# Graph attention on one core: scores laid out by unit, head and node, and gathers released unit by unit

## What is computed

```python
h = layer_norm(x, ln1_g, ln1_b)
xl = (h @ Wl + bl).reshape(n, HEADS, DIM)
xr = (h @ Wr + br).reshape(n, HEADS, DIM)
e = jax.nn.leaky_relu(xl[src] + xr[dst], NEG_SLOPE)
score = jnp.einsum('ehd,hd->eh', e, att)
smax = jax.ops.segment_max(score, dst, num_segments=n)
ex = jnp.exp(score - smax[dst])
alpha = ex / (segment_sum(ex, dst)[dst] + 1e-16)
g = segment_sum(xl[src] * alpha[..., None], dst)
x = x + (g.reshape(n, HEADS * DIM) + gat_b) @ proj_W + proj_b
x = x + gelu(layer_norm(x, ln2_g, ln2_b) @ W1 + b1) @ W2 + b2
```

## Time and profile before

| | |
|---|---|
| median of 3 runs | 3252.38 us (3250.22 to 3263.53) |
| span of the profiled execution, first to last instruction | 3186.6 us |
| median less span (what lies around the span) | 65.8 us |
| TensorE clock granted, mean | 0.897 |
| PE, weight loads, DVE, ACT, POOL busy | 77%, 50%, 45%, 43%, 48% |
| DMA | 334.02 MB, mean 105 GB/s |

### The profile page before, as it was taken

One profiled execution on the slowest core, in us unless ns is written; L12 is line 12 of the kernel. 1 busy time (PEld: TensorE's weight loads), 2 busy tenths in 40 slices (PEclk: granted clock), 3 DMA queues, 4 the chain that ended last, 5 costly groups with the idle time before them and its releaser, 6 DMA issues. The chain is left out here.

```text
span 3186.6 us, 87535 instructions
## 1 busy us (share of the span) xinstructions
PE 2458.3 (77%) x29581; PEld 1603.2 (50%) x29581; DVE 1438.1 (45%) x5714; ACT 1377.3 (43%) x3472; POOL 1539.2 (48%) x1664
## 2 busy tenths in 40 slices
PE   4678787878787787777758788777787788878775
PEld 2345555555555555555534455555455555545554
DVE  7334444444444444444543444444444443444444
ACT  4234444444444444444533444444444444444444
POOL 5655454554545454455225544455554454454440
PEclk7798999899989999999958998999999888899887
DMA  5443444444434444444224333343333333343330
GB/s 145 144 110 103 108 109 110 110 109 105 114 108 110 112 109 109 109 113 112 57 81 114 109 103 102 103 111 102 106 109 103 103 106 103 105 110 102 103 101 10
DMA packets 236833, 334.02 MB, mean 105 GB/s; under 512 B 51010, under 2 KB 160490, under 8 KB 236394
## 3 DMA queue, kind: packets, MB, share of 16 engines
q0 software_dynamic: 75072, 208.30, 24.9%
q1 hardware_dynamic: 161322, 120.16, 13.2%
HBM read 308.02 MB, written 20.25 MB: 103 GB/s over the span
## 5 line engine op out<-in xcount | busy, mean ns | idle before, releaser
L984 POOL DMA_INDIRECT rows<-table,src_t x1564 | 1488.2, 952 | 1449.6 <-PE psum L1111 1065.2
L1206 ACT ACTIVATE lz<-psum 128x512 f32<-128x512 f32 x782 | 467.1, 597 | 1632.3 <-DMA table<-row 543.2
L1092 PE MATMUL psum<-lz,att_w 128*32 128x128 f32 x6256 | 525.5, 307 | 315.2 <-issue 279.9
L1108 PE MATMUL psum<-ident,rows 128*128 128x128 f32 x3128 | 572.6, 308 | 71.6 <-issue 36.8
L1434 DVE SCALAR_TENSOR_TENSOR acc<-acc,keep,psum 128x129 f32 x782 | 273.3, 349 | 537.1 <-remote 322.4
L1108 PEld LDWEIGHTS psum<-ident,rows 128*128 128x128 f32 x3128 | 377.4, 154 | 258.2 <-issue 219.2
L1092 PEld LDWEIGHTS psum<-lz,att_w 128*32 128x32 f32 x6256 | 198.9, 113 | 491.9 <-issue 406.2
L1083 PE MATMUL psum<-ident,rows 128*32 128x128 f32 x6256 | 409.7, 302 | 35.1 <-issue 33.5
L1181 PE MATMUL psum<-rows,wgt 128*32 128x129 f32 x6256 | 317.2, 287 | 145.2 <-issue 98.8
L1330 DVE TENSOR_SCALAR oh<-relb,win_col,less 128x256 bf16<-128x256 int16 x782 | 247.6, 362 | 237.0 <-PE psum L1092 82.1
L1111 PE MATMUL psum<-oh,xrw 96*128 96x256 bf16 x1564 | 335.3, 297 | 6.6 <-DVE acc L1434 4.1
(11 more groups left out here) (256 smaller groups left out, 2169.5 us busy)
## 6 DMA issues: line engine op xcount, KB each, us to landing
xrw<-xr_split SPq DMA_DIRECT2D x782, 48.0 KB
relb<-rel_d SPq DMA_DIRECT2D x194, 192.0 KB
rows<-table,src_t POOLq DMA_INDIRECT x1564
relb<-cyc_d SPq DMA_DIRECT2D x194, 64.0 KB
xr_split<-split SPq DMA_DIRECT2D x50, 192.0 KB, 1.9
table<-row SPq DMA_DIRECT2D x50, 130.0 KB, 2.1
x_mid<-x SPq DMA_DIRECT2D x25, 64.0 KB
xo<-x_mid SPq DMA_DIRECT2D x25, 64.0 KB
```

The source lines that it names most:

```text
L984: pool.indirect_dma_start(rows[:, u % ROWS, t, :, :].rearrange("p h c -> p (h c)"), None, s["tables"][layer][0:NP, :], bass.IndirectOffset ...
L1092: m = pe.matmul(out[o:o + W, :], w["att_w"][:, h * W:h * W + W], lz[:, u % M, h * UE + t * P:h * UE + t * P + P], start=False, stop=True, ...
L1108: pe.matmul(z[:, o:o + P], rows[:, u % ROWS, t, h, 0:D], s["ident"][:, :], is_transpose=True, start=(h == 0 and t == 0), stop=False, skip_ ...
L1206: act.activation(lz[:, u % M, :], ps[u % M][:, :], ACT.Relu).then_inc(lz_ready, 1)
```

## The change

The scores of a step are laid out anew: (unit, head, node) on 128 partitions by 256 edges, so that both tiles of a unit lie side by side in columns. With that:

- `rows` becomes a ring of 10 steps, in each the two tiles, then the two units. It still has room for 20 units.
- ACT gets a new copy: the linear parts of the step's two units, repeated over 32 nodes, go into a tile `lin`. It waits for the gathers of both units, and for the score of the step before the last. PE then makes the linear part with two matmuls for a step, where there were eight.
- Mask and relu part are one and two matmuls of 256 columns for a unit, where there were two and four of 128.
- The exponential is one activation for a step, and the halves of the lowest score need no joining.
- The stations behind the score work on whole steps (`of_step`) and no more on shifted pairs, so exp, turn, weights, sums and adding each stand one place later in the lists, and the lists have one more step at the end of each layer.
- POOL waits for `z_ready` before the gathers of every unit, for the unit six before, and no more once a step.

```diff
             for u in range(NU):
-                if u >= 3 * M and u % M == 0:
+                if u >= 3 * M:
                     pool.wait_ge(z_ready, u - 3 * M + 1)
                 for t in range(K):
...
-                for t in range(K):
-                    for h in range(H):
-                        o = t * HW + h * W
-                        pe.matmul(out[o:o + W, :], rows[:, u % ROWS, t, h, D + 1:RC].to_broadcast([P, W]), s["ident"][:, :],
-                                  start=True, stop=False, skip_group_check=True)
-                for t in range(K):
-                    pe.matmul(out[t * HW:t * HW + HW, :], s["mask_w"][:, :], oh[:, u % (3 * M), t * P:t * P + P],
-                              start=False, stop=False, skip_group_check=True)
+                    pe.wait_ge(lin_ready, g + 1)
+                    for t in range(K):
+                        pe.matmul(out[0:n, t * P:t * P + P], lin[:, g % 2, t, 0:n], s["ident"][:, :],
+                                  start=(t == 0), stop=False, skip_group_check=True)
+                pe.matmul(out[at:at + HW, 0:UE], s["mask_w"][:, :], oh[:, u % (3 * M), :],
+                          start=False, stop=False, skip_group_check=True)
                 pe.wait_ge(lz_ready, u + 1)
-                for t in range(K):
-                    for h in range(H):
-                        o = t * HW + h * W
-                        m = pe.matmul(out[o:o + W, :], w["att_w"][:, h * W:h * W + W],
-                                      lz[:, u % M, h * UE + t * P:h * UE + t * P + P], start=False,
-                                      stop=True, skip_group_check=True)
+                for h in range(H):
+                    o = at + h * W
+                    m = pe.matmul(out[o:o + W, 0:UE], w["att_w"][:, h * W:h * W + W],
+                                  lz[:, u % M, h * UE:h * UE + UE], start=False, stop=True, skip_group_check=True)
...
-                old = behind(i - 6)
+                old = of_step(i - 7)
...
-                old = behind(i - 3)
-                for u in old:
-                    act.wait_ge(max_ready, i - 2)
-                    hold(act, ex_turned, i - 4)
-                    m = act.activation(ex[:, (u + 1) % (2 * M), :], hold_s[:, place(u), :], ACT.Exp,
-                                       bias=peak[:, place(u + 1):place(u + 1) + 1], scale=-1.0)
+                old = of_step(i - 4)
                 if old:
-                    m.then_inc(ex_ready, 1)
+                    n, c = len(old) * HW, (i - 4) % 4
+                    act.wait_ge(max_ready, min(i - 2, NO))
+                    hold(act, ex_turned, i - 5)
+                    act.activation(ex[0:n, (i - 4) % 2, :], hold_s[0:n, c, :], ACT.Exp, bias=peak[0:n, c:c + 1],
+                                   scale=-1.0).then_inc(ex_ready, 1)
+                new = of_step(i)
+                if new:
+                    for u in new:
+                        act.wait_ge(rows_in[u % ROWS], (u // ROWS + 1) * (16 * K))
+                    hold(act, score_ready, i - 1)
+                    act.copy(lin[:, i % 2, :, :].rearrange("p t (c w) -> p (t c) w", w=W),
+                             rows[:, ring(new[0]), :, :, :, D + 1:RC].rearrange("p t u h c -> p (t u h) c"
+                                                                                ).to_broadcast([P, K * M * H, W])
+                             ).then_inc(lin_ready, 1)
...
-                v.wait_ge(low_ready, 2 * b + 2)
-                v.tensor_copy(low2[:, :], low[HW:P, :]).then_inc(low2_ready, 1)
-                v.wait_ge(low2_ready, b + 1)
-                v.tensor_tensor(both[:, :], low[0:HW, :], low2[:, :], ALU.min).then_inc(both_ready, 1)
+                v.wait_ge(low_ready, b + 1)
+                if n == M:
+                    v.tensor_copy(low[0:HW, 1:M], low[HW:P, 0:1]).then_inc(both_ready, 1)
```

More of the change, by code:

```diff
@@ L781, in of_step, with step_of @@
     return [u for u in range(w * M, w * M + M) if 0 <= u < NU]
[L784 to L792, removed]
+def step_of(u):
+    return u // M
 def node_step(t):
-    return min(behind_of(t * TILE + 20), NO - 1) + 9
+    return min(step_of(t * TILE + 20), NO - 1) + 10
 def edge_pass(nc, sb, sem, ps, wts, s, layer):
@@ L881, in edge_pass @@
         split_out = [sem(f"split_out{i}") for i in range(2)]
-    rows = sb("rows", [P, ROWS, K, H, RC], F32)
+    rows = sb("rows", [P, ROWS // M, K, M, H, RC], F32)
+    lin = sb("lin", [P, 2, K, M * HW], F32)
     relb = sb("relb", [P, RING, UE], I16)
@@ L974, in place, with ring @@
         return u % (4 * M)
+    def ring(u):
+        return u // M % (ROWS // M)
     with nc.Block() as block:
@@ L1190, in _ @@
                         project(i * M + j)
-                    old = behind(i - 4)
-                    if j == 0 and old:
-                        pe.wait_ge(ex_ready, i - 3)
-                        hold(pe, wgt_ready, i - 4)
-                        for u in old:
-                            c = (u + 1) % M * P
-                            m = pe.transpose(ps[4][:, c:c + P], ex[:, (u + 1) % (2 * M), :], s["ident"][:, :])
+                    if j == 0 and of_step(i - 5):
+                        pe.wait_ge(ex_ready, i - 4)
+                        hold(pe, wgt_ready, i - 5)
+                        for t in range(K):
+                            m = pe.transpose(ps[4][:, t * P:t * P + P], ex[:, (i - 5) % 2, t * P:t * P + P],
+                                             s["ident"][:, :])
                         m.then_inc(ex_turned, 1)
@@ L1211, in _ @@
                     relu(new[0])
[L1212 to L1218 removed]
+                if of_step(i - 6):
+                    act.wait_ge(ex_turned, i - 5)
+                    hold(act, sums_ready, i - 7)
+                    act.copy(wgt[:, (i - 6) % 2, :, :].rearrange("p t c -> p (t c)"), ps[4][:, 0:UE]
                              ).then_inc(wgt_ready, 1)
@@ L1279, in _ @@
                 if new:
-                    o = place(new[0])
-                    n = len(new)
+                    n = len(new) * HW
                     act.wait_ge(score_ready, i - 1)
-                    hold(act, ex_ready, i - 4)
-                    act.copy(hold_s[:, o:o + n, :].rearrange("p u c -> p (u c)"), scores(i - 2)[:, 0:n * P]
-                             ).then_inc(held, 1)
-                old = behind(i - 3)
-                for u in old:
-                    act.wait_ge(max_ready, i - 2)
-                    hold(act, ex_turned, i - 4)
-                    m = act.activation(ex[:, (u + 1) % (2 * M), :], hold_s[:, place(u), :], ACT.Exp,
-                                       bias=peak[:, place(u + 1):place(u + 1) + 1], scale=-1.0)
-                if old:
-                    m.then_inc(ex_ready, 1)
+                    hold(act, ex_ready, i - 5)
+                    act.copy(hold_s[0:n, (i - 2) % 4, :], scores(i - 2)[0:n, 0:UE]).then_inc(held, 1)
+                old = of_step(i - 4)
+                if old:
+                    n, c = len(old) * HW, (i - 4) % 4
[12 more added lines that the diff above has]
+                             ).then_inc(lin_ready, 1)
                 for t in nodes(i, -2):
-                    act.wait_ge(added, min(behind_of(t * TILE + 20), NO - 1) + 1)
+                    act.wait_ge(added, min(step_of(t * TILE + 20), NO - 1) + 1)
                     hold(act, comb_ready, t - 1)
@@ L1334, in lowest @@
             def lowest(b):
-                new = of_step(b)
-                n, o = len(new), place(new[0])
+                n = len(of_step(b))
                 c = b % 8 * M + 1
```

75 lines of the change are left out of this document (34 added, 41 removed).

## The result

The changed kernel takes 2719.66 us (2717.65 to 2720.94, four runs) against 3252.69 us (3250.22 to 3263.53): a ratio of 0.836, 95% interval 0.834 to 0.838, 16.4% faster. The forecast was 3100 us with a range of 2980 to 3350: the direction was right, the size far too small, and the time lies outside the range.

A forecast was written before the change was run, and what follows sets the result against it. Bound: a step loop in which gathers hold up PE's results. 3.06 + 3.46 + 0.4 = 6.9 us against 7.30 saves 157 us over 392 steps; 3186.6 - 157 + 5 = 3035, plus 65.8 gives 3100 us, range 2980 to 3350.

The forecast's parts named there:

- the hold-up while gathers are under way: PE's results come late during a batch of four gathers and all at once after it; a quiet step takes 7.30 us.
- First and second half, 3.06 + 3.46 us: Times from each pair of gathers to the next: 3.06 us for the first, 3.46 us for the second, longer results assumed.
- The remainder, 0.4 us: Work behind the second pair that PE could not start ahead: between 0 and 1.31 us a step, taken as 0.4.
- 1.31 us: PE's free run behind the hold-up in the old step, 1551.59 to 1552.90; the upper bound of the work left over.
- I apply it to steps with node work too; their extra work stays: The quiet step's gain of 0.4 us was applied to all 392 steps, 157 us in total.
- What lies around the span, 65.8 us: Time outside the profiled span of 3186.6 us, added to 3035 us to give 3100 us.
- PE's own work, 0.0 us (-0.3 to +0.9), costed at nothing: Per step: linear part -0.20, mask -0.14, relu part +0.30 us; said to lie under the hold-up.
- ACT, DVE, the end: ACT's new copy and exponential cost nothing, DVE loses two small operations off the path, one more step per layer: +5 us.
- no change: Rival, chance 0.16: PE loses a fixed time for each gather, however batched, so 3257 us.
- Slower: Rival, chance 0.25: the whole free run falls behind the second pair; 7.8 us a step, 3460 us.
- without that cover it would cost up to 0.9: PE's changed matmul work would cost up to 0.9 us a step if the hold-up did not hide it.
- a remainder of 1.05 us: In the slower rival, somewhat past its deciding point of 0.8 us; the time was given as 3355 us.

## Why the prediction was right or wrong

- **What bounds the kernel** (the hold-up while gathers are under way): right, for the chips of the first comparison. With half of the gathers its whole cost was gone. What the prediction didn't consider is that the kernel alone doesn't bring the hold-up about: on the third chip it is absent.
- **First and second half, 3.06 + 3.46 us**: right in size, in the wrong kernel. The old layout with waits by unit shows 3.23 and 3.32 us. In the changed kernel most steps have one batch of four instead, since both projections now count 0.7 to 0.9 us apart. The prediction put a hold-up between the two counts; but in a quiet step the odd projection comes straight behind the even one and counts before the hold-up of the new batch sets in. Of the 0.7 us between 6.92 and the measured 6.22 us this is 0.3.
- **The remainder, 0.4 us**: this is the term that failed first. It had a fitting test (33 records can be started ahead, the new second half has 31) and then took a value between the bounds. In the changed kernel the remainder is 0, and 7.30 less 1.31 us is 5.99, near the 6.22 us from 1004.88 to 1011.10. At 0 the prediction's own sum gave 6.5 us and 2943 us, which is below its range. Part of the test's success is luck: the 33 of the earlier trace rows hold the six records of the odd projection, which the 31 leave out, and on the old layout with waits by unit the remainder is 0 as well, with 40 records.
- **"I apply it to steps with node work too; their extra work stays"**: wrong. From start to start of the last records of the even projections (layer 0, steps 20 to 187, by step modulo 8) the two longest steps fell from 8.84 and 8.06 us to 7.19 and 6.97, the other six from 7.2 to 7.6 us to between 4.9 and 6.7, so one of the eight gained 2.3 us and the others 0.9 to 1.7. The mean is 7.61 before and 6.34 after, a gain of 1.27 us where the sum has 0.4. A constant gain a step had no ground, and most steps have some node work. What each of these gained beyond the 1.1 us of a quiet step (7.30 to 6.22) wasn't taken apart.
- **The clock** has no term in the sum. Of these 168 steps 78 ran wholly at the full granted clock (2.4 GHz) before, and 166 do now. The 78 take 7.41 us, averaged over the eight positions, against the 7.61 of all. So up to 0.2 of the 1.27 us can be the clock; which is cause and which is effect, the long step or the low clock, isn't shown.
- **What lies around the span, 65.8 us**: wrong. It is 1.65 us, and the time of the changed kernel lies 3.7 us above its profiled span. That is 62 of the 380 us between 3100 and 2720; the steps are the rest.
- **PE's own work, 0.0 us (-0.3 to +0.9), costed at nothing**: within its bounds, at +0.42 us, and on the first kind of chip hidden or outweighed. Its terms: linear part -0.08 for -0.20, mask +0.10 for -0.14, relu part +0.40 for +0.30. What was missed is that *fewer* records are worth something by themselves: the layout alone brings 12%, though PE's time grows. By the Trainium skill (TensorE: Matmul & The Clock Gate, Part 3), small matmuls run side by side when their outputs lie in different column groups; the loss of four groups for two agrees with the relu part's 0.35 to 0.55 us, which is 0.40 of the 0.42 us that decide the case on the third chip.
- **ACT, DVE, the end**: no wait of PE for `lin` is seen, and the exponential of 256 columns takes 514 ns. From the start of the last projection's last record to the end 66.0 us, where it was 64.8; +5 us was too much.
- **The rivals**: "no change" (a fixed hold-up for each gather) falls on the first kind of chip. "Slower" fell there too, in the form told, with free work landing behind the second pair. On the third chip the change is slower, by the price that the forecast had costed at nothing: "without that cover it would cost up to 0.9". The prediction's sums have small slips as well: 6.92 and 6.52 us are taken as 6.9 and 6.5 (157 and 314 us where the terms give 149 and 306), and a remainder of 1.05 us gives 3358 us, not 3355.

The two profiles differ by 470.6 us, and nearly all of it lies in the steps: from the first projection of a layer to its last, layer 0 went from 1469 to 1238 us and layer 1 from 1475 to 1236 (1.20 us a step on the whole, since the first and last steps of a layer gain less than the 1.27 of the middle). The other 62 of the 533 us are in no profile: the profiled execution of the kernel before was quicker than its timed runs.

## What to carry to other kernels

When a stall is charged to nothing that the profile names, ask how much work the engine can start before it, count that in instructions, and compare the counts, both from the same starting point. In the changed kernel the count fitted and the whole remainder went; a value between the bounds had no mechanism behind it. Cost every edit once more with its cover gone, because the cover may be there on one chip and not on the next: the same edit was worth -16.4% and +3.8%. Of the two parts here, the waits by unit lost nothing on any chip tried, while the layout pays only where PE is held up. No version was found that is the best on both kinds.

## What the runs showed of the hardware

- While POOL issues indirect gathers, PE's results come late on some chips: 3253 us for the kernel before on two chips, 2215 us on a third, with the same 1.25 us a gather. Neither the bytes (2722.76 for 2719.66 us) nor the transfers as such (2317.91 us with plain ones for half of the gathers, 2320.28 us without these) matter, only the indirect gathers. A projection counts 0.28 us behind the start of its last record on the third chip, and 3.07 us (median of the odd ones) in the kernel before on the first kind (at most 4.3 us there, 6.2 us in the changed kernel). Whether the number of gathers decides or their standing in a row wasn't separated. What in the chip does this stays open; so does whether it belongs to the chip or to its condition at that time, as each ran within one stretch of time.
- The Trainium skill (SBUF — State Buffer, SBUF: two separate sides) holds that DMA ports and engine ports cannot contend. The third chip agrees with it, as PE runs through under the gathers; on the others the plain transfers agree too, but the indirect gathers hold PE up all the same.
- During a hold-up PE starts 33 to 38 records behind the last result that came through, and then stops: twelve one-column matmuls more (0.47 us) cost 226 us, four wide ones (0.56 us) 32 us.
- The granted clock is lower where PE pauses: 0.897 on average for the kernel before with the hold-up, 0.966 for the same kernel without.
